# A routed expert stage: gates of six of eight chunks through memory and back, in place of selector products

## The chip, the cores and the metric

One core of one Trainium2 chip runs the whole program. The metric is the device time of one execution, in microseconds, smaller being better. The numbers of the trace come from one profiled execution.

## What is computed

The reference is a decoder of two layers on x of shape (16, 128, 256), all float32: causal attention, a mixture of 8 projections chosen by table, a routed feed-forward block, banded attention, cross attention, and a block of eight experts, with a layer norm behind each. The change is in the routed feed-forward block:

```python
gs, us = flat @ wg_s, flat @ wu_s                 # 2 shared experts of width 128
out = (silu(gs) * us) @ wd_s
probs = softmax(flat @ router_w)                  # 16 routed experts of width 64
weights, indices = top_k(probs, 2); weights /= weights.sum() + 1e-9
comb = sum(one_hot(indices, 16) * weights)        # (tokens, 16), two entries are not zero
h = silu(flat @ wg_r) * (flat @ wu_r) * comb      # every expert on every token, times its gate
out = out + h @ wd_r
x = layernorm(x + out)
```

## The kernel before, in words

Each engine has its own instruction stream, ordered by hand and tied by semaphores: PE (matmuls), ACT (silu and one half of the splits), DVE (products, subtractions, norms), POOL (a few constants and powers), SP (issues the DMAs). Matmuls of full precision are made from three of a reduced one (`split3`, lines 85 to 87): both operands are split in a high and a low part.

The routed stage (`ffn_*`, from line 1146) works on four groups of four sequences, 512 tokens each. Group 0 and group 3 are written out, groups 1 and 2 are a loop. Activations lie transposed: features on the partitions, 512 tokens along the row. The 1280 hidden features are ten chunks of 128: chunks 0 and 1 are the shared experts, chunks 2 to 9 the routed ones, two experts of 64 features to a chunk. `ffn_order` writes the order of one group once for all engines:

- logits, softmax and top-2 on DVE (`router`, lines 1434 to 1451), giving the gates `comb`, tokens on partitions;
- for each chunk c: `up` on PE (gate and up projections, 12 matmuls of 512 columns), silu on ACT (L1380), and on DVE the product with the up half (L1457). For a routed chunk DVE then multiplies by the gates (L1461). ACT and DVE split the result in a high part (L1386) and a low part (L1536) for `down` (12 matmuls of 256 columns, L85 to L87), which comes two chunks later on PE: down(c-2) stands behind up(c);
- behind chunk 1, PE transposes the gates to 16 rows of 512 tokens (L1336), and DVE copies them out of PSUM as high and low part into `combT` (L1468, L1469);
- to multiply, each gate row must stand on the 64 partitions of its expert. The step "s" does that for every routed chunk: a matmul of a 0/1 selector with `combT` (`spread`, L1310) writes the two gate rows, 64 times each, to a PSUM bank, and L1461 reads them there. The selector of 8 x 128 columns is built on POOL during the mixture stage and copied once by DVE (L1396);
- at the end of a group the next group's x is transposed (L1281) out of `f3Xs`, which SP loads with one DMA a group (L1239), copied by ACT (L1369) and split by DVE (L1402). In the last group the next stage's x, keys and queries stand between the chunks instead, and wait by semaphore until selector products of chunks 6 to 9 have left the PSUM banks they share.

PE's order within a chunk of groups 1 and 2 is: up(c), selector product of c, down(c-2). At c = 10 come the transposes, down(8) and down(9). DVE's is: product and gating of c, split of c-1.

In group 0 other work is woven in: the end of the mixture (DVE L1039 to L1059), the splitting of the banded attention's weights at chunks 6 to 9 (`split_unit`, DVE L698 to L714), which SP loads (L690) as two buffers come free, and two memsets on POOL (L1256, L1257), released when DVE has done chunk 5. `combT` and the constants of `F3` live in regions laid out by hand (`Region.place`). At the end SP lays queries and keys by many DMAs (L1702) for the next stage, the first of them when DVE has split the first queries (L2044).

```python
bank = g_fill(g, ffn_spread(g, c))
...
nc.tensor.matmul(bank, F3.sel[:, c - SC, :], F3.combT[:, :], start=True, stop=True).then_inc(s["g_full"], 1)
```

Of the kernel before, what the change touches and what calls it, by code (L numbers as in the profile page):

```python
# [89 lines left out]
def program(nc, x_in, ctxT_in, itokT_in, w_a1, w_e1i, w_e1o, w_ffn, w_a4, w_a5, w_e6i, w_e6o,  # L90
# [925 lines left out]
    def mix_vector(v, c, parts, beside=None, between=None):  # L1016
# [150 lines left out]
    F3.sel32 = m2.place("f3sel32", [P, FC - SC, P], F32)  # L1167
    F3.sel = r1b.place("f3sel", [P, FC - SC, P], F32R)
    F3.s = signals("f3", "xs_loaded xt_hi g_full g_evac soft_exp comb_ready gu_full sg_ready t_done hi_ready h_ready "
                         "d_full r_done ln_var rstd_ready x_done sel_pool sel_ready")  # L1170
    assert m.at <= n_at
    FG = 2 + FC - SC + DC
# [3 lines left out]
    def ffn_order(first, last):  # L1176
# [46 lines left out]
    FL, FT, FX = 0, 1, 2 + FC - SC  # L1223
# [4 lines left out]
    def ffn_x(g, ch):  # L1228

        return (FX - 4 if ffn_last(g) else FX) + ch  # L1230

    def ffn_spread(g, c):
        return c + (DC if ffn_last(g) and c >= FC - 4 else 0)

    def ffn_sync(sp):
        s = F3.s
        with sp.Fori(1, NG) as g:
            sp.wait_ge(s["xt_hi"], g * DC + C1)
            sp.dma_start(F3.Xs[:, :, :], X[:, bass.ds(g * GB, GB), :]).then_inc(s["xs_loaded"], 16)  # L1239

    def ffn_selector_pool(pool):
# [5 lines left out]
        for n, row in enumerate((0, LO_ROWS)):  # L1247
            nc.gpsimd.affine_select(out=sel, in_=sel, compare_op=ALU.not_equal, fill=1.0, base=-row,
                                    pattern=[[-2, FC - SC], [-1, 2], [0, R_MID]], channel_multiplier=1).then_inc(s["sel_pool"], 1)
# [36 lines left out]
    def ffn_tensor(pe, first_keys, first_queries):  # L1286
# [16 lines left out]
        def spread(g, c):  # L1303

            bank = g_fill(g, ffn_spread(g, c))
            if ffn_last(g) and c >= FC - 2:
                pe.wait_ge(N.s["g_evac"], n_filled(0, NK + c - (FC - 2)))
# [50 lines left out]
        pe.wait_ge(s["sel_ready"], 1)  # L1358
        ffn_groups(pe, steps)

    def ffn_scalar(act):
# [9 lines left out]
        def steps(g, order):  # L1371
            for kind, c in order:
# [8 lines left out]
                elif kind == "h":  # L1381
                    if c < SC:
                        act.wait_ge(s["t_done"], g * FC + c + 3)
                    else:
                        act.wait_ge(s["g_evac"], ffn_evac(g, ffn_spread(g, c)))
# [27 lines left out]
    def ffn_vector_begin(v, ch):  # L1413
        s = F3.s
        if ch == 0:
            nc.vector.memset(F3.combT[:, :].bitcast(F32), 0.0).then_inc(s["sel_ready"], 1)
            nc.vector.memset(F3.pr[:, :, R_N:], -1.0).then_inc(s["sel_ready"], 1)
            v.wait_ge(s["sel_ready"], 3)
        ffn_transposed_x(v, -1, ch)

    def ffn_vector(v, link, of_mixture, following):
# [31 lines left out]
        def product(g, c):  # L1453
# [48 lines left out]
        def steps(g, order):  # L1502
            if type(g) is not int:
                link.begin(g, 1, F_LINKS)
            for kind, c in order:
# [98 lines left out]
    def n_filled(G, f):  # L1604

        return G * NF + f + 1
# [186 lines left out]
    def n_projections(pe):  # L1793
# [23 lines left out]
        def first_keys(ch):  # L1817
# [3 lines left out]
            pe.wait_ge(F3.s["g_evac"], ffn_evac(NG - 1, ffn_spread(NG - 1, FC - 4 + ch)))  # L1821
# [7 lines left out]
    def n_tensor(pe, after, projections):  # L1829
# [15 lines left out]
        def project_v(G, b):  # L1845
            c = n_of(G)
            kh, kl = of_context(G) if c.cross else of_x(G)
            if G == 0 and b < 2:
                pe.wait_ge(F3.s["g_evac"], ffn_evac(NG - 1, ffn_spread(NG - 1, FC - 2 + b)))
# [316 lines left out]
    with block as block:  # L2166
        @block.sync
        def _(sp):
# [122 lines left out]
        def _(v):  # L2291
# [51 lines left out]
            of_mixture = mix_vector(v, M2, m2, lambda: (ffn_selector(v), ffn_vector_start(v)), lambda ch: ffn_vector_begin(v, ch))  # L2343
# [77 lines left out]
```

## Time and profile before

| | |
|---|---|
| median of 3 runs | 1547.68 us (1547.19 to 1548.28) |
| the profiled execution | 1546.91 us, of which the trace spans 1544.9 us |
| busy in the span | PE 1506.9 us (98%), DVE 993.8 (64%), ACT 725.9 (47%), POOL 204.4 (13%) |
| mean granted clock of PE | 0.995 |
| moved by DMA | 66.50 MB, mean 43 GB/s |
| routed stage | about 674 to 888 us of the span |

Times of rows are in microseconds from the start of the span. A line of the timeline gives the start, the duration, the engine and line of the kernel, the operation and `out<-in`, and in brackets how long the engine stood idle before it and who released it. PE's durations overlap: a matmul is listed from its start until its last result is written, while the next is already streaming. The routed stage can be read by groups, which begin at about 674, 731, 780 and 830 us.

### The profile page before, as it was taken

What the parts mean: (1) busy time and instruction counts of PE and PEld (TensorE: products, weight loads), DVE (VectorE), ACT (ScalarE), POOL (GpSimd) and SP (SyncE); (2) the same over time, 40 slices, a digit from 0 to 9 for tenths busy, and PEclk for the clock granted to TensorE, in tenths of its full rate; (3) what the DMA queues carried; (4) which work ended last, traced back from release to release, by engine and by line L of the source; (5) the groups of instructions that cost most, each with busy time, mean ns of one, the idle gap of its engine ahead of it and who ended that gap; (6) DMA issues with size and microseconds to landing.
All of it is one profiled execution on the core that took longest, in us unless ns stands there. A gap on an engine that the chain in (4) does not pass through costs nothing.

```text
span 1544.9 us, 28583 instructions
## 1 busy us (share of the span) xinstructions
PE 1506.9 (98%) x11018; PEld 1311.1 (85%) x11018; DVE 993.8 (64%) x2131; ACT 725.9 (47%) x1874; POOL 204.4 (13%) x215
## 2 busy tenths in 40 slices
PE   7999999999999999998999999999999999999997
PEld 6988998789999999987888877777777989999996
DVE  6777777865544545576666567788887464544447
ACT  4665666622222222222233377788885444444443
POOL 1322232310000000002000033212221200000001
PEclk9999999999999999999999999999999999999999
DMA  6000100011100101000000277678760000000001
GB/s 220 1 15 2 42 2 1 29 40 36 32 28 28 53 27 39 24 11 34 1 14 1 50 103 119 82 102 115 124 97 28 10 19 28 28 27 27 27 0 54
DMA packets 43081, 66.50 MB, mean 43 GB/s; under 512 B 4577, under 2 KB 33505, under 8 KB 42849
## 3 DMA queue, kind: packets, MB, share of 16 engines
q1 hardware_dynamic: 42976, 65.09, 20.3%
q8 instruction: 68, 1.11, 0.3%
q14 instruction: 37, 0.30, 0.1%
HBM read 36.24 MB, written 2.10 MB: 25 GB/s over the span
## 4 chain that ended last, share of the span: by engine, by line
PE 90%; DVE 6%; ACT 2%; issue 1%; DMA 1%; SPq 0%; POOL 0%; DVEq 0%; POOLq 0%; ACTq 0%
PE ps L85 24%; PE ps L86 23%; PE ps L87 23%; PE ps L1880 3%; PE ps L1894 3%; PE ps L392 2%; PE ps L1925 2%; PE ps L1870 2%; PE ps L404 2%; PE ps L417 2%; PE ps L1908 1%; PE ps L1867 1%; ACT wPr L472 1%; PE ps L1916 0%; PE ps L1842 0%
## 5 line engine op out<-in xcount | busy, mean ns | idle before, releaser
L871 ACT ACTIVATE m2hT_h<-ps 128x512 fp32r<-128x512 f32 x128 | 76.8, 600 | 281.2 <-PE ps L87 281.2
L995 DVE TENSOR_TENSOR m6hT_l<-m6h,m6hT_h 128x512 fp32r<-128x512 f32 x128 | 88.6, 692 | 164.8 <-ACT m6hT_h L869 164.7
L997 DVE SCALAR_TENSOR_TENSOR m2hT_l<-ps,m2hT_h 128x512 fp32r<-128x512 f32 x128 | 88.5, 691 | 163.4 <-ACT m2hT_h L871 163.4
L868 ACT ACTIVATE m6h<-ps,m6b 128x512 f32<-128x512 f32 x128 | 88.2, 689 | 197.0 <-PE ps L87 193.0
L2006 ACT ACTIVATE nPr<-ps,negm 128x128 f32<-128x128 f32 x512 | 147.2, 384 | 24.7 <-DVE negm L2109 23.8
L87 PE MATMUL ps<-w_h,m6hT_l 128*128 128x256 f32 x512 | 144.4, 282 | 0.0
L85 PE MATMUL ps<-w_h,m6hT_h 128*128 128x256 f32 x512 | 143.5, 280 | 0.6 <-DVE m6hT_l L995 0.6
L86 PE MATMUL ps<-w_l,m6hT_h 128*128 128x256 f32 x512 | 143.7, 281 | 0.0
L87 PE MATMUL ps<-m2w_h,m2hT_l 128*128 128x256 f32 x448 | 126.8, 283 | 0.0
L86 PE MATMUL ps<-m2w_l,m2hT_h 128*128 128x256 f32 x448 | 126.7, 283 | 0.0
L85 PE MATMUL ps<-m2w_h,m2hT_h 128*128 128x256 f32 x448 | 126.3, 282 | 0.0
L2109 DVE TENSOR_REDUCE negm<-ps 128x4 f32<-128x512 f32 x128 | 88.1, 688 | 41.0 <-PE ps L1870 40.4
L905 POOL TENSOR_TENSOR rstd<-veps,mhalf 128x4 f32<-128x4 f32 (+1 forms) x9 | 10.1, 1118 | 696.2 <-DVE veps L1054 691.3
L85 PE MATMUL ps<-m6XT_h,w_h 128*128 128x512 f32 x256 | 101.5, 397 | 0.6 <-DVE m6hT_l L995 0.6
L85 PEld LDWEIGHTS ps<-w_h,m6hT_h 128*128 128x128 f32 x512 | 96.4, 188 | 6.5 <-DVE m6hT_l L995 0.9
L86 PE MATMUL ps<-m6XT_l,w_h 128*128 128x512 f32 x256 | 101.3, 396 | 0.0
L86 PEld LDWEIGHTS ps<-w_l,m6hT_h 128*128 128x128 f32 x512 | 96.4, 188 | 5.5
L87 PE MATMUL ps<-m6XT_h,w_l 128*128 128x512 f32 x256 | 100.5, 393 | 0.0
L472 ACT ACTIVATE wPr<-ps,negm 128x128 f32<-128x128 f32 x256 | 90.9, 382 | 12.2 <-DVE negm L563 12.2
L87 PEld LDWEIGHTS ps<-w_h,m6hT_l 128*128 128x128 f32 x512 | 96.2, 188 | 0.0
L85 PEld LDWEIGHTS ps<-m2w_h,m2hT_h 128*128 128x128 f32 x448 | 85.5, 191 | 4.8
L317 POOL TENSOR_TENSOR wPr<-wPr,wrec 128x512 f32<-128x512 f32 x64 | 65.9, 1051 | 178.1 <-DVE wrec L568 178.1
(322 smaller groups left out, 4331.5 us busy)
## 6 DMA issues: line engine op xcount, KB each, us to landing
nKm<-nKc_h SPq DMA_DIRECT2D x64, 128.0 KB, 4.3
nQs<-nQc_h SPq DMA_DIRECT2D x64, 128.0 KB, 5.5
raw<-in_w_e1i SPq DMA_DIRECT2D x9, 512.0 KB, 3.3
raw<-in_w_e1o SPq DMA_DIRECT2D x9, 512.0 KB, 3.3
raw<-in_w_e6i SPq DMA_DIRECT2D x9, 512.0 KB, 3.3
raw<-in_w_e6o SPq DMA_DIRECT2D x9, 512.0 KB, 3.3
nKm<-nKc_l SPq DMA_DIRECT2D x32, 128.0 KB, 4.9
nQs<-nQc_l SPq DMA_DIRECT2D x32, 128.0 KB, 5.5
```

The source lines that it names most:

```text
L85: nc.tensor.matmul(out, wh, xh, start=start, stop=False, **kw)
L86: nc.tensor.matmul(out, wh, xl, start=False, stop=False, **kw)
L87: return nc.tensor.matmul(out, wl, xh, start=False, stop=stop, **kw)
L317: nc.gpsimd.tensor_tensor(own, own, scale.unsqueeze(2).broadcast_to([P, QH, S]), ALU.mult).then_inc(s["p_ready"], 1)
L472: last = nc.scalar.activation(W.Pr[:, p % 3, half, j, :], ps[:, WSB[half], j * S:(j + 1) * S], ACT.Exp, bias=negm[:, n % 4, j:j + 1], accu ...
L868: nc.scalar.activation(c.h32[:, u % 2, :], ps[:, u % 2, :], ACT.Gelu, bias=bias)
L871: nc.scalar.activation(c.hT[0][:, ch, :], ps[:, u % 2, :], ACT.Relu).then_inc(c.s["hi_ready"], 1)
L995: last = nc.vector.tensor_tensor(c.hT[1][:, ch, :], c.h32[:, u % 2, :], c.hT[0][:, ch, :].bitcast(F32), ALU.subtract)
L997: last = nc.vector.scalar_tensor_tensor(c.hT[1][:, ch, :], ps[:, u % 2, :], 0.0, c.hT[0][:, ch, :].bitcast(F32), ALU.max, ALU.subtract)
L1880: last = nc.tensor.transpose(ps[:, TB[n % 2], i * S:(i + 1) * S], N.Pr[:, n % 4, i, :], ident[:, :])
L2006: last = nc.scalar.activation(N.Pr[:, i % 4, j, :], ps[:, SB[i % 2], j * S:(j + 1) * S], ACT.Exp, bias=negm[:, i % 4, j:j + 1])
L2109: nc.vector.reduce_max(negm[:, i % 4, :], ps[:, SB[i % 2], :].rearrange("p (h k) -> p h k", h=QH), AX.X, negate=True).then_inc(s["s_max"], 1)
```

## The change

`SL = SC + 2` divides the routed chunks. Chunks 2 and 3 keep the selector product; the selector shrinks to these two chunks. For chunks 4 to 9:

- DVE makes one more copy of the transposed gates out of PSUM, in full float32 (`combR`, 16 x 512), ahead of the copy into `combT`.
- SP stores it to a tensor in memory (`gate_rows`, 32 KB), waits for that, and then issues one DMA per chunk that reads the chunk's two rows 64 times each and writes 128 partitions of 2 KB (256 KB). There are four places in SBUF: chunks 4 and 5 have one each, chunks 6 and 8 share one, 7 and 9 another, so the last two DMAs wait until chunks 6 and 7 are gated.
- DVE's gating reads that place instead of the PSUM bank, after a wait for the DMA.

In group 0 these DMAs stand on SP's queue between the loads of the attention's weights, and the load of `f3Xs` comes behind them; in groups 1 and 2 they stand behind the load of `f3Xs` for the group to come. The copy of the selector moves from the mixture stage to DVE's stream behind chunk 0 of group 0. The selector, `combR` and two of the four places lie where the next stage's x (`nXT0`) is written in group 3; that and the freed bank order remove the waits of the next stage's first keys and values for selector products.

```diff
-    F3.sel32 = m2.place("f3sel32", [P, FC - SC, P], F32)
-    F3.sel = r1b.place("f3sel", [P, FC - SC, P], F32R)
+    SL = SC + 2
+    F3.sel32 = m2.place("f3sel32", [P, SL - SC, P], F32)
+    n_x0_at = r2.start + 45120
+    assert m.at <= n_x0_at
+    at_x0 = Region(nc, n_x0_at, 8 * KB)
+    F3.sel = at_x0.place("f3sel", [P, SL - SC, P], F32R)
+    at_x0.at = n_x0_at + 2 * KB
+    F3.combR = at_x0.place("f3combR", [P, GT], F32)
+    gates_a = at_x0.place("f3gatesa", [P, 2, GT], F32)
+    gates_b = r1b.place("f3gatesb", [P, 2, GT], F32)
+    F3.gate = [gates_a[:, i, :] for i in range(2)] + [gates_b[:, i, :] for i in range(2)]
+    F3.laid = [sem(f"f3_laid{i}") for i in range(4)]
+    gate_rows = nc.dram_tensor("gate_rows", (R_N, GT), F32).ap()
...
-                order += ([("s", c)] if c >= SC else []) + ([("nq", 0), ("nq", 1)] if queries else []) + [("t", c)]
+                order += ([("s", c)] if SC <= c < SL else []) + ([("nq", 0), ("nq", 1)] if queries else []) + [("t", c)]
...
+    def ffn_gated(g, c):
+
+        if c < SL:
+            return F3.s["g_evac"], ffn_evac(g, ffn_spread(c))
+        return F3.s["gated"], g * (FC - SL) + (c - SL + 1)
+
+    def ffn_place(c):
+
+        i = c - SL
+        return (i, 0, 1) if i < 2 else (2 + i % 2, (i - 2) // 2, 2)
+
+    def ffn_store_gates(sp, g):
+        sp.wait_ge(F3.s["rows_ready"], g + 1)
+        sp.dma_start(gate_rows, F3.combR[0:R_N, :]).then_inc(F3.s["rows_stored"], 16)
+        sp.wait_ge(F3.s["rows_stored"], g * 16 + 16)
+
+    def ffn_lay_gates(sp, g, chunks):
+        for c in chunks:
+            i, load, _ = ffn_place(c)
+            if load:
+                sp.wait_ge(*ffn_gated(g, c - 2))
+            rows2 = gate_rows[2 * (c - SC):2 * (c - SC) + 2, :]
+            sp.dma_start(F3.gate[i], rows2.unsqueeze(1).broadcast_to([2, R_MID, GT])).then_inc(F3.laid[i], 16)
 
     def ffn_sync(sp):
         s = F3.s
-        with sp.Fori(1, NG) as g:
+        sp.wait_ge(s["xt_hi"], DC + C1)
+        sp.dma_start(F3.Xs[:, :, :], X[:, GB:2 * GB, :]).then_inc(s["xs_loaded"], 16)
+        with sp.Fori(2, NG) as g:
             sp.wait_ge(s["xt_hi"], g * DC + C1)
             sp.dma_start(F3.Xs[:, :, :], X[:, bass.ds(g * GB, GB), :]).then_inc(s["xs_loaded"], 16)
+            ffn_store_gates(sp, g - 1)
+            ffn_lay_gates(sp, g - 1, range(SL, FC))
+        ffn_store_gates(sp, NG - 1)
+        ffn_lay_gates(sp, NG - 1, range(SL, FC))
...
             if c >= SC:
-                v.wait_ge(s["g_full"], ffn_full(g, ffn_spread(g, c)))
+                if c < SL:
+                    v.wait_ge(s["g_full"], ffn_full(g, ffn_spread(c)))
+                    gate, done = ps[:, 4 + c % 2, :], s["g_evac"]
+                else:
+                    i, load, loads = ffn_place(c)
+                    v.wait_ge(F3.laid[i], g * (16 * loads) + 16 * (load + 1))
+                    gate, done = F3.gate[i], s["gated"]
                 v.wait_ge(s["t_done"], g * FC + c + 3)
-                nc.vector.tensor_tensor(F3.h32[:, c % 2, :], F3.tt[:, c % 2, :], ps[:, 4 + c % 2, :], ALU.mult).then_inc(s["g_evac"], 1)
-                v.wait_ge(s["g_evac"], ffn_evac(g, ffn_spread(g, c)))
+                nc.vector.tensor_tensor(F3.h32[:, c % 2, :], F3.tt[:, c % 2, :], gate, ALU.mult).then_inc(done, 1)
+                v.wait_ge(*ffn_gated(g, c))
...
+            nc.vector.tensor_copy(F3.combR[0:R_N, :], src).then_inc(s["rows_ready"], 1)
             link(nc.vector.tensor_copy(hi, src))
...
+                    if type(g) is int and g == 0 and c == 0:
+                        ffn_selector(v)
...
                 load_unit(sp, U_A4, k, w_a4[:, at:at + n], n)
+                if k == 1:
+                    ffn_store_gates(sp, 0)
+                    ffn_lay_gates(sp, 0, range(SL, FC - 2))
+                elif k > 1:
+                    ffn_lay_gates(sp, 0, [FC - 4 + k])
```

## Rows read from the trace of the kernel before

**Rows 1.** The page: the chain that ended last, its shares by engine.
```profile
PE 90%; DVE 6%; ACT 2%; issue 1%; DMA 1%; SPq 0%; POOL 0%; DVEq 0%; POOLq 0%; ACTq 0%
```
**Rows 2.** Windows: stretch and length, busy us and (instructions) per engine, clock, DMA share, GB/s.
```profile
709.50:714.70 5.20, 0.12 (x1) 0.00 (x0) 5.13 (x4) 1.04 (x2) 3.21 (x2) 1.00 0.00 0
744.00:774.60 30.60, 30.60 (x175) 26.79 (x174) 17.64 (x34) 7.51 (x14) 1.02 (x1) 1.00 0.00 1
```
**Rows 3.** Line L1310, selector products: ns min/median/max, first and last start.
```profile
L1310 PE MATMUL ps<-f3combT,f3sel x32: 388/396/483, 686.7 to 875.7; 128*128 128x512 f32 x32
```
**Rows 4.** Timeline of PE in group 0 about one selector product.
```profile
704.79 0.40 PE L1310 MATMUL ps<-f3combT,f3sel 128*128 128x512 f32 x1
705.02 0.29 PE L85 MATMUL ps<-wF_h,f3hT_h 128*128 128x256 f32 x1
```
**Rows 5.** Line L1468, the first copy of the transposed gates, ns and starts.
```profile
L1468 DVE CAST f3combT<-ps x4: 670/672/672, 684.9 to 838.8; 16x512 fp32r<-16x512 f32 x4
```
**Rows 6.** Timeline of group 1 after the gates are copied out of PSUM.
```profile
741.05 0.67 DVE L1468 CAST f3combT<-ps 16x512 fp32r<-16x512 f32 x1
...
742.47 0.69 DVE L1536 TENSOR_TENSOR f3hT_l<-f3h,f3hT_h 128x512 fp32r<-128x512 f32 x1
...
743.72 0.29 PE L85 MATMUL ps<-wF_h,f3hT_h 128*128 128x256 f32 x1
```
**Rows 7.** Line L1396, the copy of the selector, ns.
```profile
L1396 DVE CAST f3sel<-f3sel x1: 682/682/682, 401.7 to 401.7; 128x1024 fp32r<-128x1024 f32 x1
```
**Rows 8.** Timeline of DVE at chunk 1 of group 0.
```profile
684.30 0.69 DVE L1457 TENSOR_TENSOR f3h<-f3gs,ps 128x512 f32<-128x512 f32 x1 [1.10 <-ACT f3gs L1380]
```
**Rows 9.** Line L1536, an operation with both inputs in SBUF: ns.
```profile
L1536 DVE TENSOR_TENSOR f3hT_l<-f3h,f3hT_h x40: 681/692/694, 687.5 to 880.2; 128x512 fp32r<-128x512 f32 x40
```
**Rows 10.** Timeline of DVE in group 1: chunks 4 and 9 gated, last split.
```profile
753.99 0.69 DVE L1461 TENSOR_TENSOR f3h<-f3tt,ps 128x512 f32<-128x512 f32 x1
...
776.19 0.69 DVE L1461 TENSOR_TENSOR f3h<-f3tt,ps 128x512 f32<-128x512 f32 x1
...
778.86 0.68 DVE L1536 TENSOR_TENSOR f3hT_l<-f3h,f3hT_h 128x512 fp32r<-128x512 f32 x1
```
**Rows 11.** Timeline of PE in group 1: its last down-projection.
```profile
779.60 0.39 PE L85 MATMUL ps<-wF_h,f3hT_h 128*128 128x256 f32 x1 [0.26 <-DVE f3hT_l L1536]
```
**Rows 12.** Timeline of group 0: memset, weight split, and the stall.
```profile
700.50 0.39 PE L85 MATMUL ps<-wF_h,f3hT_h 128*128 128x256 f32 x1 [0.18 <-DVE f3hT_l L1536]
...
703.77 6.94 POOL L1256 MEMSET nKm<- 96x8192 f32 x1 [2.46 <-DVEq L1525]
...
707.13 3.73 DVE L698 TENSOR_SCALAR raw<-raw 128x256 f32<-128x256 f32 x1
...
714.77 0.58 PE L85 MATMUL ps<-wF_h,f3hT_h 128*128 128x256 f32 x1 [5.15 <-DVE f3hT_l L1536]
```
**Rows 13.** Timeline of group 0: residual load issued, its transposes.
```profile
718.89 10.48 SPq L1239 DMA_DIRECT2D f3Xs<-X  x2
...
726.71 0.60 PE L1281 MATMUL ps<-ident,f3Xs 128*128 128x128 f32 x4
...
730.45 0.19 PEld L85 LDWEIGHTS ps<-wF_h,f3hT_h 128*128 128x128 f32 x1 [0.33 <-DVE f3hT_l L1536]
```
**Rows 14.** DMA issues: tile, count, KB of one, median us from issue to landing.
```profile
out<-X SPq DMA_DIRECT2D x2, 256.0 KB, 2.1
raw<-in_w_a SPq DMA_DIRECT2D x2, 128.0 KB, 2.3
```
**Rows 15.** Windows as in 2: 2 KB packets, then 4 KB packets, in the DMA engines.
```profile
115.20:115.40 0.20, 0.20 (x3) 0.20 (x4) 0.00 (x0) 0.20 (x1) 0.00 (x0) 1.00 1.09 389
...
720.00:721.00 1.00, 1.00 (x7) 0.83 (x6) 0.00 (x0) 0.21 (x1) 0.00 (x0) 1.00 0.90 363
```
**Rows 16.** Timeline of DVE in group 3: chunk 9 gated, first queries split.
```profile
877.36 0.69 DVE L1461 TENSOR_TENSOR f3h<-f3tt,ps 128x512 f32<-128x512 f32 x1
878.25 0.69 DVE L2044 TENSOR_TENSOR nQc_l<-ps,nQc_h 128x512 fp32r<-128x512 f32 x1 [0.20 <-ACT nQc_h L1969]
```

More of the change, by code:

```diff
@@ L1166, in program @@
     m2 = Region(nc, M2.end, r2.end - M2.end)
-    F3.sel32 = m2.place("f3sel32", [P, FC - SC, P], F32)
-    F3.sel = r1b.place("f3sel", [P, FC - SC, P], F32R)
+    SL = SC + 2
[11 more added lines that the diff above has]
+    gate_rows = nc.dram_tensor("gate_rows", (R_N, GT), F32).ap()
     F3.s = signals("f3", "xs_loaded xt_hi g_full g_evac soft_exp comb_ready gu_full sg_ready t_done hi_ready h_ready "
-                         "d_full r_done ln_var rstd_ready x_done sel_pool sel_ready")
+                         "d_full r_done ln_var rstd_ready x_done sel_pool sel_ready rows_ready rows_stored gated")
     assert m.at <= n_at
-    FG = 2 + FC - SC + DC
+    FG = 2 + SL - SC + DC
     LO_ROWS = 32
@@ L1221, in ffn_evac @@
         return g * FG + (DC + k + 3)
-    FL, FT, FX = 0, 1, 2 + FC - SC
+    FL, FT, FX = 0, 1, 2 + SL - SC
     def ffn_last(g):
@@ L1228, in ffn_x, with ffn_spread @@
     def ffn_x(g, ch):
-        return (FX - 4 if ffn_last(g) else FX) + ch
-    def ffn_spread(g, c):
-        return c + (DC if ffn_last(g) and c >= FC - 4 else 0)
+        return FX + ch
+    def ffn_spread(c):
+        return c - SC + 2
+    def ffn_gated(g, c):
[16 more added lines that the diff above has]
+            sp.dma_start(F3.gate[i], rows2.unsqueeze(1).broadcast_to([2, R_MID, GT])).then_inc(F3.laid[i], 16)
     def ffn_sync(sp):
         s = F3.s
-        with sp.Fori(1, NG) as g:
+        sp.wait_ge(s["xt_hi"], DC + C1)
+        sp.dma_start(F3.Xs[:, :, :], X[:, GB:2 * GB, :]).then_inc(s["xs_loaded"], 16)
+        with sp.Fori(2, NG) as g:
             sp.wait_ge(s["xt_hi"], g * DC + C1)
             sp.dma_start(F3.Xs[:, :, :], X[:, bass.ds(g * GB, GB), :]).then_inc(s["xs_loaded"], 16)
+            ffn_store_gates(sp, g - 1)
+            ffn_lay_gates(sp, g - 1, range(SL, FC))
+        ffn_store_gates(sp, NG - 1)
+        ffn_lay_gates(sp, NG - 1, range(SL, FC))
     def ffn_selector_pool(pool):
@@ L1248, in ffn_selector_pool @@
             nc.gpsimd.affine_select(out=sel, in_=sel, compare_op=ALU.not_equal, fill=1.0, base=-row,
-                                    pattern=[[-2, FC - SC], [-1, 2], [0, R_MID]], channel_multiplier=1).then_inc(s["sel_pool"], 1)
+                                    pattern=[[-2, SL - SC], [-1, 2], [0, R_MID]], channel_multiplier=1).then_inc(s["sel_pool"], 1)
             if n == 0:
@@ L1303, in spread @@
         def spread(g, c):
-            bank = g_fill(g, ffn_spread(g, c))
-            if ffn_last(g) and c >= FC - 2:
-                pe.wait_ge(N.s["g_evac"], n_filled(0, NK + c - (FC - 2)))
+            bank = g_fill(g, ffn_spread(c))
+            if type(g) is int and g == 0 and c == SC:
+                pe.wait_ge(s["sel_ready"], 3)
             if c == SC:
@@ L1356, in steps @@
                     first_queries(c)
-        pe.wait_ge(s["sel_ready"], 1)
         ffn_groups(pe, steps)
@@ L1384, in steps @@
                     else:
-                        act.wait_ge(s["g_evac"], ffn_evac(g, ffn_spread(g, c)))
+                        act.wait_ge(*ffn_gated(g, c))
                     nc.scalar.activation(F3.hT[0][:, c % 3, :], F3.h32[:, c % 2, :], ACT.Identity).then_inc(s["hi_ready"], 1)
@@ L1417, in ffn_vector_begin @@
             nc.vector.memset(F3.pr[:, :, R_N:], -1.0).then_inc(s["sel_ready"], 1)
-            v.wait_ge(s["sel_ready"], 3)
+            v.wait_ge(s["sel_ready"], 2)
         ffn_transposed_x(v, -1, ch)
@@ L1820, in first_keys @@
                 pe.wait_ge(prep_done, U_A5)
-            pe.wait_ge(F3.s["g_evac"], ffn_evac(NG - 1, ffn_spread(NG - 1, FC - 4 + ch)))
             project(0, "k", A4.wk, ch, *of_x(0))
@@ L1847, in project_v @@
             kh, kl = of_context(G) if c.cross else of_x(G)
-            if G == 0 and b < 2:
-                pe.wait_ge(F3.s["g_evac"], ffn_evac(NG - 1, ffn_spread(NG - 1, FC - 2 + b)))
             bank = g_fill("v", (G, b))
@@ L2342, in _ @@
             v.sem_inc(stage_done, 1)
-            of_mixture = mix_vector(v, M2, m2, lambda: (ffn_selector(v), ffn_vector_start(v)), lambda ch: ffn_vector_begin(v, ch))
+            of_mixture = mix_vector(v, M2, m2, lambda: ffn_vector_start(v), lambda ch: ffn_vector_begin(v, ch))
             def start_n():
```

## The prediction

> **What bounds the kernel now.** I read the page's chain of waits first: 90% of it is PE work [rows 1], so a PE instruction taken away counts if PE is not waiting for something else where it stood. The windows answer that per stretch. In group 1 of the routed stage PE is busy in all 30.60 us of the stretch from its third chunk to its last, at the full granted clock; groups 2 and 3 look the same. In group 0 there is a hole of 5.2 us with PE at 0.12 us [rows 2]. The DMA engines are all but idle in both stretches (shares of 0.00), so what they get is a new load and not contention. Then come the timelines at the places where PE waits: chunk boundaries with DVE late, and the group's end.
>
> **The matmuls removed.** There are 32 selector products, 8 a group [rows 3]; 24 go. A matmul's listed 0.40 us overlaps the next one, so the price is the distance from start to start: 704.79 to 705.02, 0.23 us [rows 4]. All 24 would be 5.5 us. Not all stand on the path:
> - Groups 1 and 2, chunks 4 to 8: PE never pauses there [rows 2], 5 x 0.23 = 1.15 us each. Chunk 9's product stands after its up-projection. From there the chain is silu on ACT, six DVE operations of 0.69 us and the last down-projection, for which PE already waits 0.26 us [rows 10, 11]. That product is worth nothing.
> - Group 3: the same 1.15 us, and 0.1 of chunk 9's: the first queries come earlier out of PE, but their split on DVE stands behind the gating of chunk 9 (877.36 plus 0.69, then 878.25) [rows 16].
> - Group 0: chunk 5's product ends in a wait for DVE (700.50), those of chunks 6 and 7 in the 5.15 us stall before 714.77, which is set by DVE's weight split, stretched to 3.73 us beside POOL's 6.94 us memset [rows 12]. They are worth nothing. Chunk 4's moves the memset and the stall's end forward by 0.23, chunk 8's is 0.23: 0.46 us together.
>
> **DVE's added work.** Each group gets one more copy of the gates out of PSUM, of the shape of the first copy: 0.67 us [rows 5]. It goes ahead of the copy that feeds the two selector products kept. In group 0 the two copies end near 686.3 and the selector product starts at 686.7 [rows 3, 5], so it comes about 0.35 us late. In group 1 that product has room, but the split of chunk 0 behind the copies moves from 742.47 to 743.14 and ends at 743.83, with 0.06 us to PE 0.17 us after the down-projection's present start at 743.72 [rows 6]. By the same reading groups 2 and 3 lose 0.2 and 0.28 us. The gate product itself reads SBUF where it read PSUM. An operation of that size with both inputs in SBUF takes 692 ns [rows 9] against 0.69 us with one in PSUM [rows 10]: no change. The selector's copy now falls between chunks 0 and 1 of group 0. It is a quarter of one that took 0.68 us [rows 7] and DVE idles 1.10 us there [rows 8]; uncovered it would cost at most 0.68 us. Where it stood before, and on POOL, nothing waited.
> Sum so far: group 0 -0.46 + 0.35 = -0.1; group 1 -1.15 + 0.17 = -1.0; group 2 -0.95; group 3 -1.25 + 0.28 = -0.97. In all **-3.0 us**.
>
> **The transfers added.** Per group one store of 32 KB and six loads of 256 KB that each read two rows 64 times ("lays" below). SP issues seven more instructions of some 0.5 us a group, and waits for four semaphores. Behind it on its queue are the residual load of the next group, two weight loads in group 0, and the laying of the first keys in group 3. The store: the shorter listed transfer to memory takes 2.1 us for 256 KB [rows 14]; 32 KB can hardly take longer, nor much less, since most of it is fixed. I take 2.1, with 0.1 for each hand-over. A lay: fixed part and packets. A 128 KB load takes 2.3 us [rows 14], of which some 0.2 to 0.4 is data, so 2.1 is fixed. The packets are the unknown.
> No row of this trace shows how a transfer is spread whose source pattern has an outer count of 2. Low end: spread over 16 engines like all the others, 256 KB at 389 GB/s in 0.7 us, each lay landing in 2.8 us and hidden; a load can't bring PE anything, so nothing lies below that. High end: cut along that outer count, so two engines carry 128 KB each. Packets of 2 KB ran at 389 GB/s over 16 engines, 24.3 GB/s an engine, thus 5.4 us; divided by the busy share of 1.09 it is 22.3 GB/s and 5.9 us, and at the 4 KB packets' 363 / (16 x 0.90) = 25.2 it is 5.2 us [rows 15]. Lays would then queue behind each other on the same two engines, whatever the other fourteen do. I take the high end, with 5.4 us: the two halves of the pattern are its only outer dimension, the copies inside it have step 0.
> The Trainium skill ("DMA: Bandwidth & Descriptors", section on why a DMA increments its semaphore by 16, and its rules for authors) says the same in stronger words: the engine count is the largest number up to 16 that divides the outermost counts of both sides, and a small outermost count confines the transfer. By it the sum is the one with two engines, +5.1 below; a spread over sixteen gives -3.0.
>
> **When the gates are there.** Group 1: rows ready at 741.05 + 0.67 = 741.7, stored at 743.9, first lay issued at 744.0. Lay n (1 to 6, for chunks 4 to 9) lands at 744.0 + 2.1 + 5.4 n: 751.5, 756.9, 762.3, 767.7, 773.1, 778.5. The fifth and sixth wait for a buffer, but are issued before the engines come free. The gating of chunk 4 starts at 753.99 and that of chunk 9 at 776.19, 4.44 us a chunk [rows 10]; with the products gone (0.23 less per chunk, 0.17 from above) chunk 9 wants its gates at 776.19 - 1.15 + 0.17 = 775.2. So chunks 4 to 6 are in time, 7 to 9 are late by 0.9, 2.1 and 3.3 us. The first two lates are mostly covered: from the end of a chunk's up-projection DVE takes 2.9 us to the split (silu 0.6, then 0.8, 0.7 and 0.7), and PE asks for it 4.2 us after that end (4.44 less 0.23), so 1.3 us are covered. The last is on the chain to the last down-projection with no room at all [rows 10, 11]: **+3.2 us** a group, in groups 1 and 2.
> Group 3 begins the same way (rows ready at 838.8 + 0.67), but its last chunks are longer, because transposes and projections of the next stage stand between: lay 6 lands at 839.5 + 2.2 + 2.1 + 32.4 = 876.2, and chunk 9 wants it at 877.36 - 1.15 + 0.28 = 876.5 [rows 5, 16]. In time.
> Group 0: the stall gives the first four lays time. Lay 5 is issued behind a weight load near 714.8 and lands at 722.3, just in time; lay 6 lands at 727.7, 1.1 late. Behind it in the two engines is a sixteenth or two of the residual load, issued at about 719.5 where it was 718.89; it lands near 728.9, and its transposes started at 726.71. Two sets of transposes (0.9 us), ACT's copy of the second (0.6, with hand-overs), and two DVE splits (1.4) bring the last down-projection to 732.1, where it is 730.45 now [rows 13]: **+1.7 us**.
> Sum: -3.0 + 3.2 + 3.2 + 1.7 = **+5.1 us**. The profiled execution took 1546.91 us (span 1544.9), the median of the runs is 1547.68; from the median I get 1552.8 us.
>
> **The rivals.**
> 1. *Two engines, 5.2 to 5.7 us a lay* (the forecast): 0.55. With 5.2 us the sixth lay is 1.2 us earlier, so +2.5; with 5.6 it is 1.2 later in groups 1 and 2 and begins to be late in group 3, about +9. Its own range is 1550 to 1557.
> 2. *Sixteen engines, every lay hidden* (not slower): 0.20. Then the sum is -3.0, 1544.7 us. The point that decides is the landing of the first lays: under 4 us each they are nowhere late. For it: the trace's 256 KB and 128 KB transfers land in 2.1 and 2.3 us [rows 14]. Against it: none of them has this pattern, and a pattern cut where it is outermost can't give more than two parts. Half of this case lies beyond 0.2%, half within.
> 3. *Two engines, but they keep pace*: 0.15. Six lays must fit in 775.2 - 746.1 = 29.1 us, 4.85 us each, 27 GB/s an engine; or store and fixed parts are shorter, or PE's room is larger, than I took. Groups 1 and 2 then lose 0 to 1.5 us each: -2.5 to +2.5, 1546.5 as its middle.
> 4. *Slower lays*: 0.10. At 5.9 us the sixth lands at 781.5, 6.3 late in groups 1 and 2, 2.7 late in group 3, group 0 +2.6: +15, 1562 us. Reading one memory row 64 times would do it, or packets of the first keys and queries held up in group 3.
>
> **How the numbers follow.** A measurement of this kernel can tell about 0.2%, 3.1 us, from no change. Slower by more: most of case 1 (0.52) and case 4, 0.62. Within: 0.03 of case 1, 0.12 of case 3, half of case 2, 0.25. Faster: the other half of case 2 and 0.03 of case 3, 0.13. The range goes from case 2's 1544.7, less 0.4 for its small terms, to 1559, which leaves out case 4's end and the better half of case 2.
>
> **What would show it.** The DMA rows: lays landing after 7.5 us for the first and over 20 us for the fourth, and a low DMA share (about 2/16) through most of each group; landings near 3 us mean case 2. DVE's gating of chunk 9 should wait for a DMA in groups 0, 1 and 2 by 1 to 4 us, and PE's last down-projection behind it. In group 0 the transposes should wait for the residual load. The window from third chunk to chunk 8 should be 1.1 us shorter per group. The store should land about 2 us after the copy. The forecast is wrong if no DVE row waits for a DMA, if the waits sit at chunk 4 (a slow store or a slow first lay), or if the time is lost outside the routed stage.

## The result and the profile after

The changed kernel takes **1553.94 us** (median of 6 runs, 1552.57 to 1554.74), the kernel before, run beside it, 1547.91 us (6 runs, 1546.87 to 1548.72). The ratio is 1.0039, with a 95% interval of 1.0029 to 1.0049: slower, by 6.0 us. Forecast were 1552.8 us (1544.3 to 1559.0) and slower.

The page of the changed kernel: its span, the chain that ended last by engine and by line, and its DMA issues (tile, count, KB, us from issue to landing).

```profile
span 1550.8 us, 28550 instructions
...
PE 86%; DVE 7%; DMA 3%; ACT 1%; issue 1%; SPq 0%; POOL 0%; DVEq 0%; POOLq 0%; ACTq 0%
PE ps L85 23%; PE ps L86 22%; PE ps L87 22%; PE ps L1928 3%; PE ps L1942 3%; DMA f3gatesb<-gate_rows 2%; PE ps L392 2%; PE ps L1973 2%; PE ps L1918 2%; PE ps L417 2%; PE ps L404 2%; PE ps L1956 1%; PE ps L1915 1%; DMA f3Xs<-X 1%; PE ps L1964 0%
...
f3gatesb<-gate_rows SPq DMA_DIRECT2D x16, 256.0 KB
```

Against [rows 1], PE's share fell from 90% to 86% and DMA's rose from 1% to 3%; two transfers stand in the chain by name, the lays (f3gatesb) and the tokens of the next group (f3Xs). The profiled span grew by 5.9 us, from 1544.9. To place it I cut the stage at the first DVE operation of each group's gating and at the first product of the next stage. The marks are rows of the timelines:

| | group 0 | group 1 | group 2 | group 3 | the rest |
|---|---|---|---|---|---|
| before | 55.76 | 49.16 | 48.94 | 56.85 | 656.09 behind |
| after | 58.01 | 51.00 | 49.47 | 58.37 | 655.63 behind |
| difference | +2.25 | +1.84 | +0.53 | +1.52 | -0.46 |

The groups make +6.1 us, the first begins 0.2 us later, and the rest behind is 0.5 us shorter; so the loss lies in the groups. The waits of the changed kernel from 674 to 905 us that a DMA ended (engine, line, releaser: us in total, times, longest us):

```profile
DVE f3h L1509 <- DMA f3gatesb<-gate_rows: 8.8, 6, 3.4
PE ps L1324 <- DMA f3Xs<-X: 1.7, 1, 1.7
```

The gatings that waited, in the timeline of DVE, with the wait in brackets, one group after the other. They answer to the gating of chunk 9 in [rows 10, 16], which waited for nothing. Chunks 8 and 9 of groups 1 and 2, then chunk 9 of group 3:

```profile
774.12 0.69 DVE L1509 TENSOR_TENSOR f3h<-f3tt,f3gatesb 128x512 f32<-128x512 f32 x1 [0.71 <-DMA f3gatesb<-gate_rows]
...
779.27 0.69 DVE L1509 TENSOR_TENSOR f3h<-f3tt,f3gatesb 128x512 f32<-128x512 f32 x1 [1.64 <-DMA f3gatesb<-gate_rows]
...
824.95 0.69 DVE L1509 TENSOR_TENSOR f3h<-f3tt,f3gatesb 128x512 f32<-128x512 f32 x1 [0.79 <-DMA f3gatesb<-gate_rows]
...
830.11 0.69 DVE L1509 TENSOR_TENSOR f3h<-f3tt,f3gatesb 128x512 f32<-128x512 f32 x1 [1.73 <-DMA f3gatesb<-gate_rows]
...
884.74 0.69 DVE L1509 TENSOR_TENSOR f3h<-f3tt,f3gatesb 128x512 f32<-128x512 f32 x1 [3.36 <-DMA f3gatesb<-gate_rows]
```

Both chunks end in a wait for their lay, so the distance between two such rows is the time of one lay: 779.27 - 774.12 = 5.15 us, and 830.11 - 824.95 = 5.16. That is 256 KB at 51 GB/s; for two engines 25.5 GB/s each, close to the 25.2 that the second of [rows 15] gives for one engine. PE, in group 1, now stands before its last down-projection for 2.15 us, where it stood 0.26 [rows 11]:

```profile
780.74 0.38 PE L85 MATMUL ps<-wF_h,f3hT_h 128*128 128x256 f32 x1 [2.15 <-DVE f3hT_l L1587]
```

Windows of the changed kernel (length, busy us per engine, granted clock, DMA share, GB/s): while the lays run in group 1, then the two stretches after that stand of PE.

```profile
746.00:779.00 33.00, 32.58 (x191) 28.41 (x189) 18.56 (x36) 9.74 (x18) 1.01 (x1) 1.00 0.13 49
...
782.00:784.00 2.00, 1.95 (x11) 1.68 (x10) 0.48 (x1) 0.00 (x0) 0.00 (x0) 0.55 0.00 0
784.00:786.00 2.00, 2.00 (x13) 2.00 (x13) 0.00 (x0) 0.00 (x0) 0.00 (x0) 0.59 0.00 0
```

The share is 0.13, two sixteenths, for 33 us at 49 GB/s. The last two rows show a second cost that I had not put in: after PE's stand its granted clock goes to its lower level, 1.2 of 2.4 GHz, for some 3.4 us if the two values are read as time at 1.0 and at 0.5. In group 2, after a stand of 2.24 us, it does not (1.00 from 832 to 836 us), and that is most of the difference between +1.84 and +0.53.

### The profile page after: what moved, and what is told of

The parts are those of the page before. It is cut to its first block, busy times and chain, and to the rows that moved or that the text cites. A ratio compares the mean times of both kernels' runs of the same rounds, so it can differ in the third digit from the quotient of the medians.

```text
span 1550.8 us, 28550 instructions
## 1 busy us (share of the span) xinstructions
PE 1504.1 (97%) x10994; PEld 1308.3 (84%) x10994; DVE 995.3 (64%) x2135; ACT 724.8 (47%) x1874; POOL 201.9 (13%) x215
## 4 chain that ended last, share of the span: by engine, by line
PE 86%; DVE 7%; DMA 3%; ACT 1%; issue 1%; SPq 0%; POOL 0%; DVEq 0%; POOLq 0%; ACTq 0%
PE ps L85 23%; PE ps L86 22%; PE ps L87 22%; PE ps L1928 3%; PE ps L1942 3%; DMA f3gatesb<-gate_rows 2%; PE ps L392 2%; PE ps L1973 2%; PE ps L1918 2%; PE ps L417 2%; PE ps L404 2%; PE ps L1956 1%; PE ps L1915 1%; DMA f3Xs<-X 1%; PE ps L1964 0%
## 5 line engine op out<-in xcount | busy, mean ns | idle before, releaser
L86 PEld LDWEIGHTS ps<-m2w_l,m2hT_h 128*128 128x128 f32 x448 | 85.5, 191 | 4.3
```

What stands on the lines that cost most here:

```text
L86: nc.tensor.matmul(out, wh, xl, start=False, stop=False, **kw)
```

## The experiments

The theory: each lay runs on two engines and takes 5.2 us. So lays queue behind each other, and whatever else uses those two engines queues behind them; without that the change would gain some 3 us. The rivals: the loss is in the extra instructions of SP and DVE, or in the passage through memory as such; or it is PE's clock. All ratios are against the kernel before, run beside each form, in brackets the 95% interval. Its median was 1548.1 us beside the first four forms, 1547.14 beside the filler in the kernel before, in the changed one and in the all-laid form, and 1548.45 beside the others. Each form has one profile, from which its groups are read.

### No store and no lays

```diff
     def ffn_store_gates(sp, g):
-        sp.wait_ge(F3.s["rows_ready"], g + 1)
-        sp.dma_start(gate_rows, F3.combR[0:R_N, :]).then_inc(F3.s["rows_stored"], 16)
-        sp.wait_ge(F3.s["rows_stored"], g * 16 + 16)
+        pass
 ...
-                    i, load, loads = ffn_place(c)
-                    v.wait_ge(F3.laid[i], g * (16 * loads) + 16 * (load + 1))
-                    gate, done = F3.gate[i], s["gated"]
+                    gate, done = F3.gate[2], s["gated"]
 ...
```

> The changed kernel without its store and its lays: DVE multiplies chunks 4 to 9 by ones from one place in SBUF, so the gates of these chunks are left out of the output. Theory (all of the loss is late lays): the terms without transfers stand alone, -3.0 us against the kernel before, 1544.9 us, and no DVE row waits for a DMA. Rival (the loss is in the added copy, the SBUF operand or the moved selector copy): still at or above the kernel before, 1548 to 1554.

1543.32 us, ratio 0.9966 (0.9954 to 0.9978), below the 1544.9 expected. The form leaves the gates of chunks 4 to 9 out of the output, and writes its ones with one memset more on DVE in group 0. Products gone and DVE's copy added, without transfers, bring 4.8 us by the medians and 3.3 by the profiled spans (1541.6 against 1544.9). The groups take 56.47, 47.65, 47.67 and 55.00 us. So the changed kernel's transfers cost 9.2 us by the spans and 10.6 by the medians, more than the whole loss.

### The same lays, each as two transfers of one row

```diff
-            rows2 = gate_rows[2 * (c - SC):2 * (c - SC) + 2, :]
-            sp.dma_start(F3.gate[i], rows2.unsqueeze(1).broadcast_to([2, R_MID, GT])).then_inc(F3.laid[i], 16)
+            for e in range(2):
+                row = gate_rows[2 * (c - SC) + e:2 * (c - SC) + e + 1, :]
+                sp.dma_start(F3.gate[i][e * R_MID:(e + 1) * R_MID, :], row.broadcast_to([R_MID, GT])).then_inc(F3.laid[i], 16)
 ...
-                    v.wait_ge(F3.laid[i], g * (16 * loads) + 16 * (load + 1))
+                    v.wait_ge(F3.laid[i], g * (32 * loads) + 32 * (load + 1))
```

> Each lay is cut into two DMAs, each of which reads one row 64 times and has 64 as its outermost count on both sides. Same bytes, same packets. Theory (two engines because the outermost count is 2): now 16 engines a DMA, a lay lands in 2.5 to 3 us, no wait of DVE or PE for them, time 1544.5 to 1545.5 us. Rival 1 (reading one memory row 64 times is what is slow): lays land as late as in the changed kernel, 8 us and more when queued, time 1553 to 1555. Rival 2 (the number of DMA instructions or SP's issue time): twice as many instructions, worse than 1554.

1544.34 us, ratio **0.9975 (0.9966 to 0.9985)**, just under what I expected. The same bytes over the same path, with twice the issues on SP, and the change is now faster than before. Its groups take 56.25, 48.08, 47.88 and 55.04 us, within 0.5 of those without any transfer. The one-row form: its DMA issues, and the gating of chunk 9 in group 1 in DVE's timeline, with no wait:

```profile
f3gatesb<-gate_rows SPq DMA_DIRECT2D x32, 128.0 KB, 3.0
f3gatesa<-gate_rows SPq DMA_DIRECT2D x16, 128.0 KB, 3.0
gate_rows<-f3combR SPq DMA_DIRECT2D x4, 32.0 KB, 1.6
```
```profile
775.55 0.69 DVE L1510 TENSOR_TENSOR f3h<-f3tt,f3gatesb 128x512 f32<-128x512 f32 x1
```

In group 1 the two terms of the work can be read apart. From the group's mark to the gating of chunk 4 it is 20.33 us where it was 20.13: the added copy, forecast at 0.17. From there to the gating of chunk 9 it is 21.07 where it was 22.20: five products, forecast at 1.15.

Reading one row of memory 64 times is thus not slow, nor is the passage through memory. The rivals of the extra instructions and of the passage fall.

### Each row stored twice, an outer count of 4

```diff
-    gate_rows = nc.dram_tensor("gate_rows", (R_N, GT), F32).ap()
+    gate_rows = nc.dram_tensor("gate_rows", (2 * R_N, GT), F32).ap()
 ...
-        sp.dma_start(gate_rows, F3.combR[0:R_N, :]).then_inc(F3.s["rows_stored"], 16)
+        sp.dma_start(gate_rows.rearrange("(e t) s -> e t s", t=2), F3.combR[0:R_N, :].unsqueeze(1).broadcast_to([R_N, 2, GT])).then_inc(F3.s["rows_stored"], 16)
 ...
-            rows2 = gate_rows[2 * (c - SC):2 * (c - SC) + 2, :]
-            sp.dma_start(F3.gate[i], rows2.unsqueeze(1).broadcast_to([2, R_MID, GT])).then_inc(F3.laid[i], 16)
+            rows4 = gate_rows[4 * (c - SC):4 * (c - SC) + 4, :]
+            sp.dma_start(F3.gate[i], rows4.unsqueeze(1).broadcast_to([4, R_MID // 2, GT])).then_inc(F3.laid[i], 16)
```

> The rows are stored twice (64 KB), and each lay reads four rows 32 times each: outermost count 4, half as many repeats of one row. Theory: four engines, 2.6 us of data a lay, the sixth lands some 15 us earlier than with two, so no late lay in groups 1 to 3 and no wait in group 0: 1544.5 to 1546 us. Rival 1 (repeats of one row): gains at most by the halved repeats; if a repeat costs, half of the loss stays, 1549 us.

1543.56 us, ratio 0.9972 (0.9963 to 0.9981), a little below what I expected, groups 56.31, 48.09, 47.86 and 55.13 us, no wait for a lay. The number of transfers and the bytes of a lay are the changed kernel's; the outer count is 4, and the store carries 64 KB in 2.4 us for 32 KB in 1.6. It is the outer count that decides. The windows show the engines too (length, busy us per engine, granted clock, DMA share, GB/s): the same five microseconds of group 1, while lays run, in the changed kernel and in this form.

```profile
750.00:755.00 5.00, 5.00 (x29) 4.39 (x28) 3.38 (x7) 1.12 (x2) 0.00 (x0) 1.00 0.13 48
```
```profile
750.00:755.00 5.00, 5.00 (x30) 4.33 (x29) 4.49 (x14) 1.11 (x2) 1.02 (x1) 1.00 0.26 102
```

The share is four sixteenths where it was two, and the rate twice as high.

### Four lays a group in place of six

```diff
-    SL = SC + 2
+    SL = SC + 4
 ...
-        return (i, 0, 1) if i < 2 else (2 + i % 2, (i - 2) // 2, 2)
+        return 2 + i % 2, i // 2, 2
 ...
```

> Still the changed kernel's two-row pattern, but only chunks 6 to 9 by lays (two places, so the third and fourth wait for chunks 6 and 7 to be gated), chunks 2 to 5 by selector products. Theory: two engines keep pace with four lays of 5.2 us, apart from the fourth, which needs chunk 7 gated first and lands within 1 us of its use; kept gain per group 0.5 us (three products on the path less the added copy), so 1546 to 1548.5 us; in group 3 the fourth shares the engines with the first keys and may be 1 to 3 us late. Rival (a two-row lay costs by itself, whatever the queue): four sixths of the loss, 1552 us.

1550.85 us, ratio 1.0019 (1.0010 to 1.0028), above what I expected. Groups 1 and 2 fall to 48.66 and 48.24 us, 0.5 and 0.7 under before, as expected. Groups 0 (58.79) and 3 (58.72) are no shorter than with six (58.01 and 58.37). The four-lay form: the wait of PE in group 0, and the gating of chunk 9 in group 3.

```profile
PE ps L1324 <- DMA f3Xs<-X: 2.4, 1, 2.4
```
```profile
881.28 0.69 DVE L1513 TENSOR_TENSOR f3h<-f3tt,f3gatesb 128x512 f32<-128x512 f32 x1 [3.40 <-DMA f3gatesb<-gate_rows]
```

In those groups the number of lays is not what counts. What counts is that the last ones stand in the same engines as another load: the next group's tokens in group 0, the next stage's keys in group 3. The next two experiments take these one at a time.

### The tokens' load ahead of the last two lays of group 0

```diff
-        sp.wait_ge(s["xt_hi"], DC + C1)
-        sp.dma_start(F3.Xs[:, :, :], X[:, GB:2 * GB, :]).then_inc(s["xs_loaded"], 16)
 ...
                 elif k > 1:
+                    if k == 2:
+                        sp.wait_ge(stage_done, 2)
+                        sp.wait_ge(F3.s["xt_hi"], DC + C1)
+                        sp.dma_start(F3.Xs[:, :, :], X[:, GB:2 * GB, :]).then_inc(F3.s["xs_loaded"], 16)
                     ffn_lay_gates(sp, 0, [FC - 4 + k])
-            sp.wait_ge(stage_done, 2)
```

> The changed kernel, with the load of group 1's tokens (f3Xs) issued in group 0 ahead of the last two lays and not behind all six. Theory (a transfer on the two engines of the lays waits behind them): the tokens land well before the transposes want them, the wait of PE for f3Xs (1.7 us in the changed kernel) goes, group 0 is about 1.7 us shorter, everything behind is as it was: 1551 to 1552.5 us against 1553.9. The gates of chunk 9 in group 0 may come up to 1 us later, since SP issues one thing more ahead of them. Rival (group 0 is long for another reason, its wait for h of chunk 5 and the low granted clock behind it): the wait goes, and group 0 stays within 0.5 us of the changed kernel's 58.0: 1553.4 to 1554.

A miss by its time: 1555.37 us, ratio 1.0047 (1.0033 to 1.0061), not told apart from the changed kernel's 1.0039, and group 0 takes 58.22 us. The wait of PE for f3Xs is gone, as expected. But in its place DVE waits 2.00 us for the last lay of group 0, where it waited 0.53, and 0.70 for the one before it. The gating of chunk 9 in group 0, in this form and in the changed kernel:

```profile
728.58 0.69 DVE L1507 TENSOR_TENSOR f3h<-f3tt,f3gatesb 128x512 f32<-128x512 f32 x1 [2.00 <-DMA f3gatesb<-gate_rows]
```
```profile
728.39 0.69 DVE L1509 TENSOR_TENSOR f3h<-f3tt,f3gatesb 128x512 f32<-128x512 f32 x1 [0.53 <-DMA f3gatesb<-gate_rows]
```

The order in the queue only chooses who waits. Neither version has room for both.

### The keys held until chunk 9 of group 3 is gated

```diff
                     sp.sem_inc(waited_sp, 1)
+                    if x == 0:
+                        sp.wait_ge(F3.s["gated"], NG * (FC - SL))
                     lay_keys(0, 0, x)
```

> The changed kernel, with the first lay of the keys of the next stage held in group 3 until VectorE has gated chunk 9. Theory (the keys' lays share the two engines of the sixth lay, which makes it 3.4 us late in group 3): VectorE's wait for the gates of chunk 9 in group 3 falls from 3.36 us to that of groups 1 and 2 (1.6 to 1.7 us), and group 3 ends about 1.7 us earlier, unless the keys, which now start some 8 us later, hold the next stage: then its first product waits for them, and the sum is worse than the changed kernel's. Rival (the sixth lay is late by itself in group 3): the wait stays at 3 to 3.5 us.

The gating of chunk 9 in group 3 now starts at 881.61, where it was 884.74 in the changed kernel, and without a wait. With the keys held:

```profile
881.61 0.69 DVE L1509 TENSOR_TENSOR f3h<-f3tt,f3gatesb 128x512 f32<-128x512 f32 x1
```
```profile
PE ps L1917 <- DMA nQs<-nQc_h: 8.7, 1, 8.7
```

All of the 3.36 us was the keys' doing, more than the 1.7 I expected of it. And holding them is worse: PE waits 8.7 us for the queries behind them, and the only run of this form took 1556.82 us. The sixth lay would be in time by itself, as forecast; the company of the keys is what made it late.

### Filler products in PE's idle time, three times

Group 0 without transfers is 0.5 to 0.7 us longer than before, though six products are out of it. The windows of the one-row form (as above) show why; in before the clock was 0.94 from 713 to 715 us, 0.50 to 717, 0.70 to 719 and 1.00 behind:

```profile
709.00:711.00 2.00, 0.39 (x2) 0.00 (x0) 1.97 (x2) 1.11 (x2) 2.00 (x2) 1.00 0.00 0
711.00:713.00 2.00, 0.00 (x0) 0.00 (x0) 2.00 (x1) 0.00 (x0) 1.75 (x1) 0.86 0.00 0
713.00:715.00 2.00, 0.19 (x1) 0.19 (x2) 1.86 (x4) 0.00 (x0) 0.00 (x0) 0.50 0.00 0
715.00:717.00 2.00, 2.00 (x10) 2.00 (x11) 1.83 (x4) 0.00 (x0) 0.00 (x0) 0.50 0.53 177
...
719.00:721.00 2.00, 2.00 (x10) 1.62 (x9) 0.00 (x0) 0.00 (x0) 0.00 (x0) 0.94 0.54 170
```

From 717 to 719 us it is 0.50 too. Read as time at 1.0 and at 0.5, the lower clock lasts from 712.4 to 719.2 us here, and from 714.8 to 718.2 in before. PE works again from 714.81 us in the one and from 714.77 in the other [rows 12]: 4.4 against 3.4 us at half speed, half a microsecond of work lost, which is what group 0 is longer by. The edit, in the one-row form; the changed kernel and the all-laid form get the same lines, the kernel before one wait more, for the gating of chunk 6, since the products write a bank that it uses:

```diff
         def down(g, c):
+            if type(g) is int and g == 0 and c == 5:
+                for _ in range(20):
+                    nc.tensor.matmul(ps[:, 4, :], wgu[0][:, 0, 0:P], F3.XT[0][:, 0, :], start=True, stop=True)
```

> The one-row form (1544.3 us), with 20 products of 512 columns that nothing reads, into a free bank, in the idle time of PE ahead of down(5) in group 0. Theory (the stretch at the lower clock after that idle time is what keeps group 0 from being shorter than before): the granted clock stays at 1.00 from 711 to 721 us, and group 0 (56.25 us) is 1 to 2 us shorter: 1542.5 to 1543.5 us. Rival (group 0 is set by VectorE's work in that stretch, not by PE's clock): the clock stays up and group 0 is within 0.4 us of 56.25; or the products outlast the wait and it is longer.

1542.52 us, ratio **0.9965 (0.9952 to 0.9977)**, the fastest form of all. Group 0 falls from 56.25 to 54.21 us. One-row form with the filler, the same two stretches:

```profile
713.00:715.00 2.00, 1.34 (x6) 0.76 (x5) 1.97 (x3) 0.00 (x0) 0.17 (x1) 1.00 0.00 0
715.00:717.00 2.00, 1.76 (x13) 1.74 (x14) 1.76 (x4) 0.00 (x0) 0.00 (x0) 1.00 0.38 128
```

The clock stays up. But does that gain belong to the change? The same filler in the kernel before:

> The kernel before, with the same 20 unread products in the idle time of PE (5.15 us) ahead of down(5) in group 0. Theory (PE's lower clock after that idle time costs 2 us in the one-row form): here the stretch at the lower clock is half as long (715 to 719 us), so the gain is about half of the 2.04 us of the one-row form: group 0 55.76 to 54.8 us or less, 1546.6 to 1547.3 us against 1548.1. Rival (the filler brings nothing to the kernel before, since VectorE sets its pace there): group 0 within 0.3 us of 55.76, 1548.

1544.54 us, ratio 0.9981 (0.9972 to 0.9990). By its time a miss: I expected 1546.6 to 1547.3. Group 0 falls by 1.35 us, from 55.76 to 54.41, where about 1 was expected: PE's 3.4 us at the lower clock lost 1.7 us of work, and most of that comes back. Group 3 is 0.66 us shorter as well, where the filler changes nothing; between the medians lie 2.6 us, and I can't place the rest. With the clock held up in both, group 0 is 54.21 us with the change (one-row form) and 54.41 without it: -0.2, where I had forecast -0.1.

And in the changed kernel:

> The changed kernel with the same 20 unread products. Theory of two parts in group 0 (the lower clock behind the idle time, and the lays and f3Xs on two engines): the clock part goes, the lays now come due earlier, so that VectorE's wait for the gates of chunks 8 and 9 in group 0 grows from 0.5 to 1.5 to 3 us in all, and group 0 falls by 0.3 to 1.2 us only (one-row form: 2.04): 1552.7 to 1553.6 us against 1553.9. Rival (group 0 is long through the clock alone): group 0 falls by 2 us, 1552.

1554.55 us, ratio 1.0044 (1.0030 to 1.0057): nothing gained, less than even the theory of two parts gave (1552.7 to 1553.6). The clock is 1.00 from 709 to 721 us, and yet group 0 takes 58.61 us; without the filler it took 58.01 in the changed kernel and 59.26 in the form with the keys held, whose group 0 is the same code. The changed kernel with the filler, two gatings of group 0 and its wait for tokens:

```profile
722.25 0.69 DVE L1512 TENSOR_TENSOR f3h<-f3tt,f3gatesb 128x512 f32<-128x512 f32 x1 [1.37 <-DMA f3gatesb<-gate_rows]
...
728.13 0.69 DVE L1512 TENSOR_TENSOR f3h<-f3tt,f3gatesb 128x512 f32<-128x512 f32 x1 [3.09 <-DMA f3gatesb<-gate_rows]
```
```profile
PE ps L1324 <- DMA f3Xs<-X: 3.5, 1, 3.5
```

All that PE gains is handed to the waits: chunk 8 waits 1.37 us where it waited for nothing, chunk 9 waits 3.09 us where it waited 0.53, PE 3.5 for its tokens where it waited 1.7. The two lay engines set the end of group 0, and they don't care for PE's clock. So the lays cost more in group 0 than their waits in the changed kernel show: 58.61 - 54.21 = 4.4 us at the full clock, one profile of each.

### All eight chunks laid, without and with the filler

```diff
-    SL = SC + 2
-    F3.sel32 = m2.place("f3sel32", [P, SL - SC, P], F32)
+    SL = SC
 ...
-        return (i, 0, 1) if i < 2 else (2 + i % 2, (i - 2) // 2, 2)
+        return (i, 0, 1) if i < 2 else (2 + i % 2, (i - 2) // 2, 3)
 ...
```

The lays are transfers of one row here, and DVE no longer makes the high and low part of the gates.

> All eight routed chunks by lays, each lay as two transfers of one row each (so that each uses 16 engines), no product of a selector left, and the selector and the high and low parts of the gates not made. Theory (a lay on 16 engines is hidden, and each product left costs its 0.23 us times two a group): about 4 groups x 2 chunks x 2 x 0.23 = 3.7 us less than the six-chunk form if all of PE's time counts, half of that if VectorE sets the pace of the first chunks: 1540.5 to 1542.5 us against 1544.3. Rival (the first chunk's gates come too late when they must pass the chip's memory: store 1.6 us, lay 2.5 us, after the row copy): VectorE waits for the gates of chunk 2 in each group, some 1 to 2 us, and the time is 1544 to 1548.

1544.99 us, ratio 0.9978 (0.9969 to 0.9987): with all eight products a group gone, no better than with six. The 1540.5 to 1542.5 expected were missed, and the rival came true. With the filler:

> The form with all eight chunks laid by one-row transfers, plus the 20 unread products. Theory: the filler's gain (1.8 to 2 us) adds to the all-laid form (1545.0): 1542.7 to 1543.3 us, no better than the one-row form of six chunks with the filler (1542.5), since the wait for the first lay's gates (2.1 us a group) takes what the two products left cost. Rival (each product left costs): 1540.5 to 1541.5 us.

1543.14 us, ratio 0.9974 (0.9963 to 0.9984), against 0.9965 (0.9952 to 0.9977) for six chunks and the filler: not told apart. The two products left are hardly worth removing. The all-laid form, gating of chunk 2 in group 1, and then PE:

```profile
746.69 0.69 DVE L1507 TENSOR_TENSOR f3h<-f3tt,f3gatesa 128x512 f32<-128x512 f32 x1 [1.77 <-DMA f3gatesa<-gate_rows]
```
```profile
748.16 0.39 PE L85 MATMUL ps<-wF_h,f3hT_h 128*128 128x256 f32 x1 [0.48 <-DVE f3hT_l L1582]
```

The first gates come too late through memory by 1.8 us (up to 2.7 in the other groups), and in group 1 0.48 of that reaches PE, which is what the two products had cost it (2 x 0.23).

## Why the prediction was right

It was right in its sign, its time (1.1 us under the measured one) and its main mechanism. By its own steps:

**The lays run on two engines** (rival 1, chance 0.55): shown, by 5.15 us between two landings, by a share of 0.13 for 33 us, and by the two forms that change the outer count. The trace agrees with the page of the Trainium skill that the prediction named ("DMA: Bandwidth & Descriptors", its rules for authors): an outermost count of 2 confines the lay (share 0.13), one of 4 to twice as many engines (share 0.26), and a row of its own, like that, frees it enough. Rival 2 (sixteen engines, 1544.7 us) is what the one-row form makes true: 1544.34 us.

**Work without transfers, -3.0 us.** By groups, the one-row form against before gives -1.08 and -1.06 us in groups 1 and 2, for which -1.0 and -0.95 were forecast, and in group 1 both terms came out by themselves. Group 0 gives -0.2 at a held clock (forecast -0.1), and +0.5 with the clock as it falls. Group 3 gives -1.8 (forecast -0.97); but before with the filler takes 56.19 us there, 0.66 less than before without it, so part of this is what one profile differs from another; with the filler in both it is -0.7 (55.48 against 56.19). By the medians the one-row form is 3.8 us faster, by the spans 2.4.

**Lateness in groups 1 and 2, +3.2 us each.** Too large, in its sizes and not in its mechanism. Against the one-row form the lays cost 2.9 us in group 1 and 1.6 in group 2. A lay took 5.2 us and not 5.4, so that the sixth is 1.2 us earlier, and the store 1.6 us and not 2.1 (0.5): 3.2 - 1.7 = 1.5 us, which is group 2. The 5.2 stood in the text, as an end of the range; the 1.6 did not. Group 1 has 1.3 us more, from the lower clock after PE's stand, a term that I didn't have. Whether a group pays it differs by profile: four profiles have the same code in these two groups (the changed kernel, with the filler, with the tokens' load moved, with the keys held), and there group 1 takes 51.00, 50.78, 50.84 and 49.64 us, group 2 49.47, 50.56, 50.61 and 50.72.

**Group 3, "in time".** Wrong: the one step that failed in kind. The sixth lay was due in time, but the keys of the next stage were issued from 873.16 us on and, by the two experiments on order, shared its engines, and DVE waited 3.36 us. With them held it waited for nothing. I had counted what SP's queue must pass, and had left what shares the engines to rival 4. It cost 3.3 us against the one-row form (58.37 - 55.04).

**Group 0, +1.7 us through the tokens' load.** PE waited 1.7 us for it, and the group is 1.8 us longer than in the one-row form. The sixth lay was 0.53 us late, for which 1.1 was forecast. The size agrees, though partly by chance: the lower clock, which both forms have, covers part of the lateness; without it the same lays cost 4.4 us.

The main mechanism gave the sign. That the sum came within 1.1 us was luck, since two errors cancelled: some 1.7 us too much in each of groups 1 and 2, against 3.3 us too little in group 3, with group 1's clock (1.3 us) on the side of the loss as well.

## What to carry to other kernels

Look at the outermost count of a transfer before its bytes: a pattern "two rows, 64 copies" ran on two engines (5.2 us, and queued), while two transfers of one row each landed in 3.0 us, and this turned a change that lost 0.39% into one that gained 0.25%. When a transfer is confined to few engines, list every other load of the same time, since each has a share in those engines; moving it in the queue only moves the wait. And look at the clock behind PE's long waits: 20 filler products in one of them won 0.2% in the kernel before, about as much as the change in its repaired form.

## What was not expected of the hardware

- **The clock falls after a stand of PE of about 2 us, but not each time.** After 2.15 us in group 1 of the changed kernel the granted clock was 0.55 from 782 to 784 us; after 2.24 us in group 2 it stayed at 1.00. With the keys held, on the same code, it stayed at 1.00 in group 1 (780 to 788 us) after 2.14 us and fell in group 2 after 2.35. In the four profiles with this code it fell after six of the eight stands. The runs here don't show what decides.
- **A small shift of work lengthens the stretch at the lower clock.** The idle time ahead of down(5) grew from 5.15 to 5.4 us, and PE then worked at the lower clock for 4.4 us in place of 3.4. Taking 0.46 us of PE work out of group 0 (by the forecast's sum) made it longer by 0.5 us, in this form and in the one with rows stored twice; with the kernel before there is one profile to set against them.
- **SP itself is held up when lays pile up.** The issue of a lay took 0.5 us at best, but up to 5.4 us in the changed kernel (ns, minimum, median and maximum), when three earlier ones had just been issued. In the one-row form the issues into the same tile took 0.9 us at most, into the other 1.2:

```profile
L1270 SPq DMA_DIRECT2D f3gatesb<-gate_rows x16: 482/1552/5367, 688.7 to 870.9; - x16
```

What stands behind it on SP waits too; no run here had something there that was urgent.
